# One more of eight input products on VectorE instead of GpSimd, in a selective-scan kernel

## What is computed

```
def step(h, inp):
    dt_t, B_t, C_t, x_t = inp
    dA = jnp.exp(dt_t[..., None] * A)
    dBx = dt_t[..., None] * B_t[:, None, :] * x_t[..., None]
    h = dA * h + dBx
    y = jnp.einsum('bdn,bn->bd', h, C_t)
    return (h, y)
```

## Time and profile before

| | |
|---|---|
| median of 3 runs | 15738.19 us (15737.39 to 15739.81) |
| the profiled execution, its own time | 15743.65 us |
| its span from first to last instruction | 15741.8 us |
| busy: GpSimd, VectorE | 14373.3 us (91%), 14038.0 us (89%) |
| busy: TensorE, ScalarE | 11460.2 us (73%), 9875.8 us (63%) |
| mean granted clock of TensorE | 0.816 of full speed |
| state products L908 (2048), input products L900 (1024) on GpSimd | 4536 and 4530 ns each |
| scans L781 with and without carry (7168, 1024) | 1265 and 1206 ns each |
| input products L768 on VectorE (1024) | 2262 ns each |

### The profile page before, as it was taken

One profiled execution on the slowest core, in us unless ns is written; L12 is line 12 of the kernel. 1 busy time (PEld: TensorE's weight loads), 2 busy tenths in 40 slices (PEclk: granted clock), 3 DMA queues, 4 the chain that ended last, 5 costly groups with the idle time before them and its releaser, 6 DMA issues.

```text
span 15741.8 us, 147189 instructions
## 1 busy us (share of the span) xinstructions
PE 11460.2 (73%) x32388; PEld 3366.9 (21%) x32388; DVE 14038.0 (89%) x11204; ACT 9875.8 (63%) x15964; POOL 14373.3 (91%) x3332
## 2 busy tenths in 40 slices
PE   2777777777777777777777777777777777777777
PEld 1222222222222222222222222222222222222221
DVE  1999999999999999999999999999999999999998
ACT  5666666666666666666666666666666666666666
POOL 1999999999999999999999999999999999999999
PEclk9888788888888888888887888888888878888887
DMA  5555545555555555455555555455555555555554
GB/s 208 122 128 123 127 119 127 125 125 127 122 127 124 129 122 127 119 127 123 127 125 125 123 125 131 120 126 121 129 122 129 125 125 123 123 130 122 125 122 114
DMA packets 1035848, 1990.51 MB, mean 126 GB/s; under 512 B 120065, under 2 KB 121146, under 8 KB 1030714
## 3 DMA queue, kind: packets, MB, share of 16 engines
q1 hardware_dynamic: 1034810, 1979.41, 51.9%
HBM read 1626.62 MB, written 352.32 MB: 126 GB/s over the span
## 4 chain that ended last, share of the span: by engine, by line
POOL 34%; issue 29%; DVE 11%; PE 9%; DMA 8%; ACT 7%; SPq 2%; DVEq 0%; POOLq 0%; ACTq 0%
POOL hq L908 23%; POOL dbx L900 10%; DVE hq L781 5%; DMA dtx_d<-sp 3%; DMA dtx_rep<-dtx_d 3%; PE pp L332 2%; ACT ps_a L574 1%; PE ps_acc L422 1%; PE pp L375 1%; DVE gmv L797 1%; DVE dbx L768 1%; PE pp L381 1%; DVE gmv L806 1%; PE pp L389 1%; SPq L255 1%
## 5 line engine op out<-in xcount | busy, mean ns | idle before, releaser
L908 POOL TENSOR_TENSOR hq<-hq,c_rep 128x2048 f32<-128x2048 f32 x2048 | 9242.7, 4536 | 947.1 <-ACT carry L580 947.1
L781 DVE TENSOR_TENSOR_SCAN hq<-ps_a,carry,dbx 128x512 f32<-128x512 f32 x7168 | 8679.5, 1265 | 573.3 <-POOL dbx L900 329.7
L574 ACT ACTIVATE ps_a<-dt_rep,A_neg 128x512 f32<-128x512 f32 x8192 | 5575.4, 687 | 4916.4 <-DVE hq L781 4902.2
L900 POOL TENSOR_TENSOR dbx<-dtx_rep,b_rep 128x2048 f32<-128x2048 f32 x1024 | 4638.7, 4530 | 24.2 <-DMA dtx_rep<-dtx_d 24.2
L422 PE MATMUL ps_acc<-hq,dsum 128*32 128x512 f32 x16384 | 2480.5, 681 | 1219.8 <-POOL hq L908 1219.6
L768 DVE TENSOR_TENSOR dbx<-dtx_rep,ps_b 128x2048 f32<-128x2048 f32 x1024 | 2316.6, 2262 | 32.3 <-DMA dtx_rep<-dtx_d 30.9
L332 PE MATMUL pp<-xin,diag 128*128 128x504 f32 (+3 forms) x4608 | 2282.7, 614 | 12.8 <-DMA xin<-in_x 12.8
L410 PE MATMUL ps_b<-dbl,bsel 41*128 41x512 f32 x2048 | 1427.4, 783 | 294.7 <-DVE dbx L768 294.6
L366 PE MATMUL pp<-x,W_taps 128*128 128x512 f32 x768 | 690.2, 997 | 1065.1 <-DVE x L744 1065.1
L781 DVE TENSOR_TENSOR_SCAN hq<-ps_a,dbx 128x512 f32<-128x512 f32 x1024 | 1189.1, 1206 | 71.9 <-POOL dbx L900 55.0
L332 PEld LDWEIGHTS pp<-xin,diag 128*128 128x128 f32 x4608 | 772.7, 189 | 1535.5 <-issue 1522.6
(11 more groups left out here) (116 smaller groups left out, 10566.1 us busy)
## 6 DMA issues: line engine op xcount, KB each, us to landing
dt_rep<-dt_d SPq DMA_DIRECT2D x2048, 256.0 KB, 4.5
dtx_rep<-dtx_d SPq DMA_DIRECT2D x2048, 256.0 KB, 5.9
c_rep<-bc_d SPq DMA_DIRECT2D x1024, 256.0 KB, 5.5
b_rep<-bc_d SPq DMA_DIRECT2D x1024, 128.0 KB, 2.9
dt_d<-dt SPq DMA_DIRECT2D x256, 512.0 KB, 2.8
dtx_d<-sp SPq DMA_DIRECT2D x256, 512.0 KB, 5.9
out<-o SPq DMA_DIRECT2D x128, 512.0 KB, 3.5
xin<-in_x SPq DMA_DIRECT2D x192, 320.0 KB, 8.5
```

Source lines behind the costliest of these rows:

```text
L574: A(ps_a[:, i % RA, :], dt_rep[:, q // NQ, g, :], ACT.Exp, scale=A_neg[:, q // NQ, q % NQ, g:g + 1]).then_inc(exp_done, 1)
L781: v.tensor_tensor_scan(hq[:, q % HQ, g, :], ps_a[:, i % RA, :], dbx[:, slot(q), g, :], carry[:, q, g:g + 1] if c % CH else 0.0, ALU.mult, ...
L900: g.tensor_tensor(dbx[:, slot(q), :, :], dtx_rep[:, d, :, :], b_rep[:, c % 2, q % NQ // 2, :].unsqueeze(1).to_broadcast([P, DG, T]), ALU.m ...
L908: g.tensor_tensor(quad, quad, c_rep[:, c % 2, q % NQ, :].unsqueeze(1).to_broadcast([P, DG, T]), ALU.mult).then_inc(cmul_done, 1)
```

## The change

Group 7 of each piece changes hands. VectorE makes the products of groups 0, 2, 4, 6 and 7, GpSimd of 1, 3 and 5. VectorE's product of group 7 stands after scan 24. TensorE has to fill `ps_b` once more: it selects group 7 at step 24, where it selected group 0 of the next piece, and that one moves to step 26. The semaphore counts (`bmul_dve`, `bmul_pool`, `bsel_mm`) follow, and SyncE waits for other counts before it overwrites `dtx_rep`. The DMAs stay, the row of B for group 7 in `b_rep` too, which nobody reads now.

```diff
+BY_DVE = (0, 2, 4, 6, 7)
+BY_POOL = (1, 3, 5)
+ND, NP = len(BY_DVE), len(BY_POOL)
...
# SyncE, before it spreads dt*x of the next piece
-                    sp_e.wait_ge(bmul_dve, (b * CH + c - 1) * (QUADS // 2) + 2 * (d + 1))
+                    sp_e.wait_ge(bmul_dve, (b * CH + c - 1) * ND + sum(q // NQ <= d for q in BY_DVE))
...
-                    sp_e.wait_ge(bmul_pool, (b * CH + c - 1) * (QUADS // 2) + 2 * (d + 1))
+                    sp_e.wait_ge(bmul_pool, (b * CH + c - 1) * NP + sum(q // NQ <= d for q in BY_POOL))
...
# TensorE
                     if g == 0 and s % 2 == 0:
                         if s + 2 < QUADS:
                             select_b(b, c, s + 2)
-                        elif c + 1 < end:
-                            select_b(b, c + 1, 0)
+                        else:
+                            select_b(b, c, 7)
+                    if u == 26 and c + 1 < end:
+                        select_b(b, c + 1, 0)
...
# VectorE, weigh_inputs
-                if not (isinstance(n, int) and n < 2):
+                if not (isinstance(n, int) and n < 4):
+                    dve.wait_ge(scan_done, DG * (n - (3 if q % 2 else 1)))
+                elif n >= 2 and q % 2 == 0:
                     dve.wait_ge(scan_done, DG * (n - 1))
...
# VectorE, chunk
                     scan(b, c, u)
+                    if u == 24:
+                        weigh_inputs(b, c, 7)
...
# GpSimd, chunk
-                    if s % 2 == 0:
+                    if s + 1 in BY_POOL:
                         weigh_inputs(b, c, s + 1)
```

More of the change, by code:

```diff
@@ L405, in select_b @@
             def select_b(b, c, q):
-                n = (b * CH + c) * (QUADS // 2) + q // 2
+                n = (b * CH + c) * ND + BY_DVE.index(q)
                 pe.wait_ge(dbl_done, b * CH + c + 1)
@@ L539, in evac_dbl @@
                     act.wait_ge(bc_out, 16 * (b * CH + c - 1))
-                    act.wait_ge(bsel_mm, (b * CH + c - 1) * (QUADS // 2))
+                    act.wait_ge(bsel_mm, (b * CH + c - 1) * ND)
                 A(dbl[0:NDBL, c % 2, :], pp[0:NDBL, 0, :], ACT.Copy).then_inc(dbl_done, 1)
@@ L761, in weigh_inputs @@
                 d = q // NQ
-                dve.wait_ge(bsel_mm, (b * CH + c) * (QUADS // 2) + q // 2 + 1)
+                dve.wait_ge(bsel_mm, (b * CH + c) * ND + BY_DVE.index(q) + 1)
                 if q % NQ == 0:
@@ L774, in scan @@
                 if g == 0:
-                    dve.wait_ge(bmul_pool if q % 2 else bmul_dve, (b * CH + c) * (QUADS // 2) + q // 2 + 1)
+                    if q in BY_DVE:
+                        dve.wait_ge(bmul_dve, (b * CH + c) * ND + BY_DVE.index(q) + 1)
+                    else:
+                        dve.wait_ge(bmul_pool, (b * CH + c) * NP + BY_POOL.index(q) + 1)
                     if not (isinstance(m, int) and m < HQ):
```

## The result

The kernel with the change takes 15326.74 us (median of 4 runs, 15288.44 to 15389.13) beside 15737.79 us before: ratio 0.974, 95% interval 0.971 to 0.978. The forecast was 15321. Its profiled execution took 15357.84 us, its span 15356.0. The total is right; two of its terms are wrong by about 6 us an image each, with opposite signs, and the experiments are mostly about these two.

The account below looks back on a forecast made before the run. GpSimd was taken to bound ordinary pieces at 56.11 us, with VectorE at 54.75 afterwards. Per image -13.1 us over 31 images, -407, and another -10, from 15743.65 gave 15327, less 5.5 for the median: 15321 us, range 15185 to 15500.

Parts of the forecast that it names:

- GpSimd no longer bounds the ordinary piece: Ordinary pieces: GpSimd's list loses one 4.47 us input product, falls from 56.11 to 51.6 us, and GpSimd then waits.
- VectorE's list is 54.75 us: Each ordinary piece: VectorE's 53.56 us plus 2.18 for the new product, less 0.99 for y's covered wait.
- The next four ... -5.39: Pieces 2 to 5 of an image: 224.39 us becomes 4 x 54.75 = 219.0, a change of -5.39 us.
- The select of group 7 in time: TensorE's new select ends before VectorE's group 7 product: no wait in an ordinary piece, 0.4 us in piece 8.
- Piece 6, L785 "waits one operation", together -1.59: Piece 6: the diagonals' product waits out one GpSimd operation, 5.65 us for 8.43; with +1.19, -1.59 us.
- L785 slips in: Rival, piece 6: the diagonals' product goes ahead of GpSimd's state product and costs 1.36 us; 15188 us, chance 0.10.
- Piece 8, -6.25: Piece 8: waits vanish, 2.18 and 0.4 us are added, L797 falls from 5.92 to 0.22; sum -6.25 us.
- the rival that it stays locked: Rival, piece 8: L797 still waits for a GpSimd state product, up to 5.7 us an image; 15498 us, chance 0.10.
- Slower by TensorE's clock: Rival: TensorE at 1.2 GHz delays sum and select, group 7 product waits 6 us; +340, 15660 us, chance 0.06.
- No gain, waits of 1.6 us behind those that vanish: Rival: other VectorE waits, for ScalarE or TensorE, take 1.6 us a piece that piece 1 hides; 15738 us, chance 0.04.

Follow-up runs that it names:

- r2: Changed kernel with VectorE's group 7 product made for one column of 512 only (group 7's numbers wrong): 15138.0 us, ratio 0.962.
- r3: Changed kernel with VectorE's group 7 product one place later, behind the y product instead of ahead of it: 15939.5 us, ratio 1.013.
- r10: Changed kernel with the group 7 product behind the y product and the first z product issued three times: 15469.1 us, ratio 0.983.
- r4: Changed kernel with TensorE's first z product issued three times instead of once, same result: 15250.5 us, ratio 0.969.
- r8: Changed kernel with the diagonals' product (two SBUF operands) made just ahead of norm and add in piece 6: 15331 us, one run.
- r5: Kernel before the change, with one operand of three one-column statistics instructions (L797, L806, L808) taken from PSUM instead of SBUF: 15635.8 us, ratio 0.993.
- r11: Changed kernel with first z product issued three times, statistics operands in PSUM, diagonals' product behind scan 26 of the piece before: 14877.6 us, ratio 0.946.

## Why the prediction was right, and which steps of it were not

- **GpSimd no longer bounds the ordinary piece.** Right. It is busy for 51.81 us of the short piece above, forecast 51.6, and it waits for the carry, 1516.0 us in all.
- **VectorE's list is 54.75 us.** Right as a floor: piece 1 measures 54.76, and 53 ordinary pieces take 54.7 to 55.1. The product costs 2.18 less the 0.99 of y's wait; r2 gives 1.1 for the difference, r3 and r10 give 1.0 for the wait.
- **"The next four ... -5.39."** This step failed: +0.66. The step behind it was to read VectorE's waits off piece 1 and take them for all pieces. Piece 1 has its x-projection at the full clock in every trace. In the others TensorE's 2.86 us idle before the second z product is followed in 37 of 120 by a low clock on the x-projection, +3.3 us, and in 29 by one on the z product and the sum, +1.7 (most of these are the 56.4 us pieces). Before, that idle time was at most 1.48 us, so no row of before could show what it costs; that the change would lengthen it is the step that the prediction lacks. r4 shows the cause: without the long idle time these pieces are at 54.87, which would have been 4 x 54.87 - 224.18 = -4.7.
- **The select of group 7 in time.** Right. L777 waits 25.1 us in all, 22.1 of them for a DMA, so at most 3.0 us over 1280 products are for selects; the 0.4 in piece 8 did not come.
- **Piece 6, L785 "waits one operation", together -1.59.** This term failed the other way: -7.08. The two times of the forecast, 10.50 and 10.44 us, were a tie, and the tie went to VectorE in 26 of 31 images. That is the rival with 0.10, "L785 slips in", priced at 4.3 us an image. The 5.5 us over the forecast are 3.6 of it (4.3 in 26 of 31) and 1.8 by which the mean piece 6 before, 65.59, lay above the 63.78 that I used. In the five other images the product took 5.65 to 5.74, as forecast.
- **Piece 8, -6.25.** Measured -5.66. L797 fell free, as forecast; the rival that it stays locked is out in every image.
- **Slower by TensorE's clock.** The condition was right and came true, in over one piece in four, but the place was wrong. I had it delay the sum of group 3 and the select, 6 us a hit; it acts on the x-projection and reaches VectorE through ScalarE's queue at 3.3 us. I had weighed only the matmuls that the new product depends on, not those that every piece depends on. Its sum is also wrong: the +340 is worked out against the kernel before and belongs on 15738, not on 15321, which gives about 16080 in place of 15660.
- **No gain, waits of 1.6 us behind those that vanish.** This is what pieces 2 to 5 did. They did it by the clock; with it kept up (r4) they gain. It did not reach the total, as pieces 1 and 6 to 8 still gave 12.4 us an image, 5.5 more than forecast in piece 6.

So the total stands on 15321 partly by luck: -5.4 us where +0.7 came, -1.6 where -7.1 came. With the clock kept up (r4) the ordinary pieces are as forecast, but piece 1 pays 2 us for the matmuls that do it.

The Trainium skill (Perfetto Trace Analysis, "Optimizing Scalar/DVE Operations") says of moves between these two engines that they "might not help". Here it helped by 2.6%: the product that moved reads one operand from the accumulation memory and runs at 2262 ns beside a busy GpSimd, as before the change.

## What to carry to other kernels

When the engine that set the pace loses work, list what each of the others waits for in a piece that the old bound did not hold, and look at more than one such piece: an idle gap of TensorE ahead of a chain through two engines can cost more than the work moved, and it can be filled with matmuls that nobody reads. Put a two-SBUF operation of VectorE where GpSimd waits; when its position is a tie by the row, price both outcomes. When one locked operation is freed, check whether the next of its kind takes the lock over.

## What the runs showed of the hardware

- An edit in one piece changed TensorE's clock in others: shortening piece 8 alone took the low x-projections from 37 to 95 of 120, and ordering two VectorE instructions the other way took the loss to nearly every piece (118 of 120 over 57 us) and the kernel from 0.978 to 1.013 of before.
- A VectorE operation with two SBUF operands can stand through three GpSimd operations (11.59 us for 128x1, 0.16 us otherwise) and can also go in at the first boundary (r8, 3.65 us). The carry that GpSimd's next operation needs had ended 0.8 us before VectorE asked in the earlier trace rows, and 0.07 us after it asked in r5 (8029.46 against 8029.39); both times GpSimd went on. In r8 it ended 1.6 us after (8185.00 against 8183.40), and VectorE went in. What decides at a boundary stays open; no run was made for it.
- Where both start at once it is decided by little. In r10 GpSimd's state product started 0.12 to 0.14 us before the diagonals in 12 of 31 images, and the diagonals waited each time (5.57 to 5.60 us); in the 19 with both starts within 0.03 us they went first in 14. In the changed kernel they went first in 26 of 30 such cases.
- The Trainium skill (SBUF — State Buffer, "SBUF: two separate sides") has whichever starts first take the pair for the whole instruction. The rows of r11, of r8 and of the tie agree: 1.33 us when GpSimd is idle, and 5.6 to 5.8 us for a state product that comes second. In the 11.59 us of r5, though, three GpSimd operations ran one after the other while VectorE waited, two of them started after it had asked.
